# Two-layer graph attention on one core: other orders of the same instructions inside a tile's step

## What is computed

```python
h = jnp.maximum(_layernorm(x, axis=-1), 0.0)
x = x + _L0_gnn_ref(h, adj, L0_gnn_W, L0_gnn_a)   # scores leaky_relu(s1[:, None] + s2[None, :])
h = jnp.maximum(_layernorm(x, axis=-1), 0.0)
x = x + _L1_gnn_ref(h, adj, ...)                  # scores q @ k.T / sqrt(d)
# both: softmax over adj > 0, times the value rows, then elu
```

## Time and profile before

| | us |
|---|---|
| median of 3 runs | 2040.26 (2037.29 to 2045.88) |
| time of the profiled execution | 2041.44 |
| its span in the profile | 2039.7 |
| first phase | to about 1090 us |
| layer 1, even stretch | about 1180 to 2000 us |

### The profile page before, as it was taken

One profiled execution on the slowest core, in us unless ns is written; L12 is line 12 of the kernel. 1 busy time (PEld: TensorE's weight loads), 2 busy tenths in 40 slices (PEclk: granted clock), 3 DMA queues, 4 the chain that ended last, 5 costly groups with the idle time before them and its releaser, 6 DMA issues.

```text
span 2039.7 us, 23050 instructions
## 1 busy us (share of the span) xinstructions
PE 1260.7 (62%) x5314; PEld 968.6 (47%) x5362; DVE 1285.1 (63%) x6912; ACT 770.2 (38%) x1507; POOL 1130.4 (55%) x1206
## 2 busy tenths in 40 slices
PE   2756766766776676676653355666666665665566
PEld 1433444444444444444443245555555655555555
DVE  4556777767777777777775255565555565565555
ACT  2865566565656665656621011111111111111111
POOL 1345555555555555555563656666666666666661
PEclk9876777676677766767755566666665566666665
DMA  9788989998899998998621211222221222222121
GB/s 314 288 308 319 324 310 331 318 333 288 321 335 322 322 331 306 334 327 315 239 56 39 57 43 49 53 53 52 55 54 53 54 53 53 54 54 53 47 55 31
DMA packets 122262, 372.40 MB, mean 183 GB/s; under 512 B 34577, under 2 KB 67858, under 8 KB 89362
## 3 DMA queue, kind: packets, MB, share of 16 engines
q1 hardware_dynamic: 75458, 289.83, 38.7%
q0 software_dynamic: 38464, 81.08, 15.3%
q10 hardware_dynamic: 8208, 0.03, 0.2%
HBM read 358.12 MB, written 12.72 MB: 182 GB/s over the span
## 4 chain that ended last, share of the span: by engine, by line
DVE 46%; another core or an unknown queue 25%; PE 11%; issue 9%; ACT 5%; DMA 2%; SPq 1%; POOL 0%; DVEq 0%; ACTq 0%; POOLq 0%
DVE arena L873 8%; PE psum L1389 4%; DVE arena L699 3%; DVE arena L758 3%; ACT arena L1171 3%; DVE arena L761 2%; DVE arena L1120 2%; DVE arena L791 2%; DVE arena L866 2%; DVE arena L891 1%; DMA table<-arena 1%; PE psum L1526 1%; PE psum L1527 1%; DVE arena L1124 1%
## 5 line engine op out<-in xcount | busy, mean ns | idle before, releaser
L572 POOL DMA_INDIRECT arena<-table,arena x576 | 549.1, 953 | 432.9 <-DVE arena L827 269.7
L602 POOL DMA_INDIRECT arena<-table,arena x576 | 553.0, 960 | 335.1 <-DVE arena L882 165.5
L1171 ACT ACTIVATE arena<-arena 128x2048 bf16<-128x2048 int32 x256 | 485.4, 1897 | 26.1 <-DMA arena<-in_adj_dram 26.0
L1349 PE MATMUL psum<-arena 128*128 128x512 bf16 x976 | 331.8, 484 | 114.5 <-ACT arena L1171 59.2
L1396 PE MATMUL psum<-arena 128*128 128x131 f32 (+1 forms) x768 | 207.6, 442 | 302.5 <-DVE arena L866 274.3
L1396 PEld LDWEIGHTS psum<-arena 128*128 128x128 f32 x768 | 172.9, 324 | 317.2 <-issue 316.7
L873 DVE SCALAR_TENSOR_TENSOR arena<-arena 128x131 f32<-128x131 f32 (+1 forms) x768 | 268.5, 350 | 36.8 <-DVE arena L876 15.5
L1349 PEld LDWEIGHTS psum<-arena 128*128 128x128 bf16 x1024 | 116.8, 124 | 286.7 <-issue 177.7
L1306 ACT ACTIVATE arena<-psum 128x384 f32<-128x384 f32 x64 | 31.5, 492 | 493.5 <-remote 456.3
L1389 PEld LDWEIGHTS psum<-arena 128*128 128x128 f32 x768 | 148.2, 273 | 90.5 <-DVE arena L856 63.9
L1389 PE MATMUL psum<-arena 128*128 128x1 f32 x768 | 141.5, 300 | 66.5 <-DVE arena L856 52.4
(11 more groups left out here) (199 smaller groups left out, 2230.0 us busy)
## 6 DMA issues: line engine op xcount, KB each, us to landing
arena<-in_adj_dram SPq DMA_DIRECT2D x256, 1024.0 KB
arena<-table,arena POOLq DMA_INDIRECT x1152
table<-arena POOLq DMA_DIRECT2D x32, 132.0 KB, 5.3
arena<-table SPq DMA_DIRECT2D x64, 66.0 KB
table<-arena SPq DMA_DIRECT2D x16, 256.0 KB
arena<-table SPq DMA_DIRECT2D x64, 64.0 KB
out_dram<-arena SPq DMA_DIRECT2D x16, 256.0 KB
arena<-in_x_dram SPq DMA_DIRECT2D x4, 0.5 KB, 12.1
```

The lines of the kernel that those rows point to most:

```text
L572: pool.indirect_dma_start(Gt[:, v % GROUP, c + 1, :], None, table0, bass.IndirectOffsetOnAxis(idx_now[:, v % GROUP, c:c + 1], 0))\
L602: pool.indirect_dma_start(Gt[:, t % GROUP, c + 1, 0:D], None, table1, bass.IndirectOffsetOnAxis(idx_now[:, t % GROUP, c:c + 1], 0))\
L1171: nc.scalar.activation(mask[:, k, q * QUARTER:(q + 1) * QUARTER], adj_sb[:, k, q, :], ACT.Relu, accum_out=sum_all[:, bass.ds(tile, 1), q:q ...
L1349: nc.tensor.matmul(V[k], shifted[:, s, :], mask[:, k, s * 512:(s + 1) * 512], start=(s == 0), stop=False)
```

## The change

The same instructions run in other orders; none is added, removed or resized, and no transfer moves to another queue. In layer 1: VectorE runs `total` ahead of `maxima`; TensorE runs `scatter` right behind the transpose of the sums and the owners' six matmuls last; ScalarE copies the transposed sums first and the owners' product last. In the first phase: ScalarE copies the dealt list behind quarter 2 instead of ahead of it, and `prob_over` goes to the head of the next step; VectorE puts `below` behind `pick`, `finish` and `measure`, and `weigh` behind the next scores; TensorE runs `scatter` and the dealing ahead of `sum_up`.

```diff
@@ VectorE, first phase @@
                     u, v, w = t - LATE, t - PICK, t - DONE
-                    if live(t, DONE):
-                        weigh(w, w % 2, w % GROUP)
...
                         score0(u, u % 2, u % GROUP, u // GROUP + 1)
+                    if live(t, DONE):
+                        weigh(w, w % 2, w % GROUP)
...
-                    if live(t, LATE):
-                        below(u, u % 2)
                     if live(t, PICK):
                         pick(v, v % GROUP)
                     if live(t, DONE):
                         finish(w, w, w % 2)
                         measure(w, w % GROUP)
+                    if live(t, LATE):
+                        below(u, u % 2)
@@ VectorE, layer 1 @@
+                        if live(t, 3):
+                            total(T + t - 3, m, DE)
                         if live(t, 2):
                             maxima(T + t - 2, k, r)
-                        if live(t, 3):
-                            total(T + t - 3, m, DE)
@@ ScalarE, first phase @@
+                    if live(t, DONE):
+                        prob_over(w, w % 2)
                     quarter(1)
+                    quarter(2)
                     if live(t, PICK):
                         act.wait_ge(deal_done, v + 1)
                         nc.scalar.activation(owned_list[:, v % GROUP, :, :], deal_ps[v % 2], ACT.Identity).then_inc(owned_done, 1)
-                    quarter(2)
...
-                    if live(t, LATE):
-                        prob_over(u, u % 2)
@@ TensorE, first phase @@
-                    if live(t, DONE):
-                        at_least(pe, summed, w - 1)
-                        sum_up(w, w % 2, w % GROUP, D + 3)
                     if live(t, LATE):
                         scatter(u, u % 2, u % GROUP)
...
                         last.then_inc(deal_done, 1)
+                    if live(t, DONE):
+                        at_least(pe, summed, w - 1)
+                        sum_up(w, w % 2, w % GROUP, D + 3)
```

More of the change, by code:

```diff
@@ L1303, in attend @@
                               .then_inc(accn_done, 1)
-                        if live(t, 1):
-                            act.wait_ge(own_done, t)
-                            nc.scalar.activation(owned[:, (b - 1) % GROUP, :, :], own_ps[(b - 1) % 2], ACT.Identity)\
-                              .then_inc(owned_done, 1)
+                            act.wait_ge(acc_turned, t - 3)
+                            nc.scalar.activation(accT[:, k, :], accT_ps[k], ACT.Identity).then_inc(accT_done, 1)
                         if live(t, 0):
@@ L1310, in attend @@
                             nc.scalar.activation(h_col[:, b % 2, :], h_col_ps, ACT.Identity).then_inc(h_col_sb, 1)
-                        if live(t, 4):
-                            act.wait_ge(acc_turned, t - 3)
-                            nc.scalar.activation(accT[:, k, :], accT_ps[k], ACT.Identity).then_inc(accT_done, 1)
-                        if live(t, 2):
-                            prob_rows(T + t - 2, k)
                         if live(t, 4):
@@ L1320, in attend @@
                         if live(t, 2):
+                            prob_rows(T + t - 2, k)
                             prob_over(T + t - 2, k)
+                        if live(t, 1):
+                            act.wait_ge(own_done, t)
+                            nc.scalar.activation(owned[:, (b - 1) % GROUP, :, :], own_ps[(b - 1) % 2], ACT.Identity)\
+                              .then_inc(owned_done, 1)
                 unrolled(attend, G + 1)
@@ L1508, in attend @@
                             nc.tensor.transpose(accT_ps[k], accn[:, k, :], ident[:, :]).then_inc(acc_turned, 1)
+                        if live(t, 2):
+                            scatter(T + t - 2, k, r)
+                        if live(t, 0):
+                            pe.wait_ge(self_in[b], 16 * (G + g + 1))
+                            at_least(pe, u_kept, t)
+                            nc.tensor.transpose(h_col_ps, Gt[:, b, 0, 0:D], ident[:, :]).then_inc(h_col_done, 1)
+                        if live(t, 4):
+                            pe.wait_ge(accT_done, t - 3)
+                            nc.tensor.matmul(o_ps[k], accT[:, k, :], proj[:, 1, :], start=True, stop=False)
+                            nc.tensor.matmul(o_ps[k], ones[0:1, 0:P], bvrow[0:1, :], start=False, stop=True).then_inc(o_done, 1)
+                        if live(t, 0):
+                            pe.wait_ge(h_col_sb, t + 1)
+                            nc.tensor.matmul(u_ps, h_col[:, b % 2, :], mix[:, 1, :], start=True, stop=True).then_inc(u_done, 1)
+                        if live(t, 2):
+                            spread_max(T + t - 2, k, r)
                         if live(t, 1):
@@ L1517, in attend @@
                             last.then_inc(own_done, 1)
-                        if live(t, 0):
-                            pe.wait_ge(self_in[b], 16 * (G + g + 1))
-                            at_least(pe, u_kept, t)
-                            nc.tensor.transpose(h_col_ps, Gt[:, b, 0, 0:D], ident[:, :]).then_inc(h_col_done, 1)
-                        if live(t, 2):
-                            scatter(T + t - 2, k, r)
-                        if live(t, 4):
-                            pe.wait_ge(accT_done, t - 3)
-                            nc.tensor.matmul(o_ps[k], accT[:, k, :], proj[:, 1, :], start=True, stop=False)
-                            nc.tensor.matmul(o_ps[k], ones[0:1, 0:P], bvrow[0:1, :], start=False, stop=True).then_inc(o_done, 1)
-                        if live(t, 0):
-                            pe.wait_ge(h_col_sb, t + 1)
-                            nc.tensor.matmul(u_ps, h_col[:, b % 2, :], mix[:, 1, :], start=True, stop=True).then_inc(u_done, 1)
-                        if live(t, 2):
-                            spread_max(T + t - 2, k, r)
                 unrolled(attend, G + 1)
```

## The result

The changed kernel takes 2178.93 us (2175.77 to 2182.32) against 2038.78 us (2035.83 to 2045.88), a ratio of 1.0682 with a 95% interval of 1.0649 to 1.0716: slower by 140 us (139 by the ratio). The profiled execution has a span of 2180.6 us, 140.9 more than before.

What follows compares the result with a forecast made beforehand. Layer 1 was taken as a loop of waits on TensorE results held during gathers, the first phase as several resources near their limit. 2041.4 - 63 (layer 1) - 15 (first phase) = 1963, forecast 1960 us, range 1885 to 2130.

Steps and rivals of the forecast that it cites:

- What bounds the kernel now: Layer 1: TensorE results finished late in nine gathers arrive about 1.9 us after the last; loop 13.8 us a tile.
- The limit at x = 6.5: Layer 1: TensorE results finished before 6.5 us into a run of gathers get through; later ones are held.
- The change in layer 1: Layer 1: two tiles take 25.4 us, a tile 12.7 instead of 13.75; 63 us off over 60 tiles.
- It is released at 11.2 + 1.9 = 13.1, if the next run doesn't matter.: Layer 1: `scatter`, held from x = 7.5, comes 1.9 us behind its run's gathers, 1.5 us into the next run.
- Rival (c): Layer 1: gather runs without a pause make it slower, 2075 us in a small case or 2200 in a large; chance 0.32.
- large case: Layer 1: a hold lasts through a second run, 16.7 us a tile, 180 us slower, 2200 us; chance 0.15.
- Rival (a): Layer 1: no hold in the new order, GpSimd bounds at 11.55 us a tile; 1880 us in all; chance 0.16.
- Rival (b): Layer 1: `total` held in every tile through `sum_up`, step 13.6 us, no change that can be told, 2030 us; chance 0.22.
- The change in the first phase: First phase: buffers come free sooner and VectorE's wait at L860 shrinks; 15 us off, between 0 and 60.
- The new wait at `weigh`: First phase: `weigh` waits for `prob_over`, now behind a mask; 1.2 us shows in every second tile.
- The range: Whole kernel: 1885 to 2130 us, leaving out the best half of (a) and most of the large case of (c).

Runs made afterwards that it cites:

- A: First stage of the staged kernel, held: layer 1 with all orders as in the kernel before; 13.6 us a tile.
- the staged kernel: Changed kernel with layer 1 cut into six stages, each with its own orders or gathering stops; held, 2120.9 us beside 2020.3 of the kernel before.
- D: Stage of the staged kernel, held: against the orders before, only TensorE's and ScalarE's new orders in layer 1; 16.3 us a tile.
- E: Stage of the staged kernel, held: changed orders, and gathers of tile t also wait for `below` of tile t - 3; 16.2 us a tile.
- the other three held traces: Changed kernel with gathers also waiting for `maxima` (2159.7 us), the staged kernel (2120.9), and seven stages with pauses or no gathers (1946.0).

## Why the prediction was wrong

**What bounds the kernel now** held up: in the held condition a pause decides when TensorE's late results arrive, and A of the staged kernel has the step of before, 13.6 us. The limit at x = 6.5 was drawn too sharp, and time in the run alone doesn't set it. `scatter` at x = 6.2 came 2.3 us late in D, so there is a stretch in which results are late but not held; `spread_max` at x = 7.9 came 1.3 us late in E. What decides between the two stays open.

**The change in layer 1.** The first half of the sum came out: owners at 4.6 (4.4 in the sum), `sum_up` at 5.9 (6.0), next run at 11.3 without a pause (11.55); only `total` was at 9.2 instead of 7.9, which cost nothing. The step that failed is "It is released at 11.2 + 1.9 = 13.1, if the next run doesn't matter." The next run matters: 1474.01 in the timeline, x = 19.95 and not 13.1. What follows from 13.1, a pause of some 2.7 us in every second tile and 12.7 us a tile, fell with it: the pause in every second tile is 10.8 us. Measured: 16.55 us and a loss of 163.8 us where 63 off were forecast.

**Rival (c)** was what happened, in its large case: 33.4 us for two tiles worked out, 33.1 measured, 2200 us against 2179. It is right in its place and size, and partly by luck in its way: I had `scatter` held to 24.7 and everything behind it free. It came at 19.95, and `spread_max` was then held to 25.7. I gave this case 0.15. Its evidence, the joined runs of the earlier trace rows with a hold to 5.9 us behind four tiles' gathers, was the only row of layer 1 that showed joined runs. I overlooked that the first phase has two runs of eighteen (127.78 to 177.56 us), and that `scatter` and the dealt lists came 3.0 us behind the second of them. There they had ended only near its end, so they say nothing of a hold that lasts through a second run. What I set against it, that a held `sum_up` makes a pause, assumed the release at 13.1 that was in question.

**Rival (a)** describes the free condition: GpSimd's 11.5 us a tile. The Trainium skill, "SBUF — State Buffer", section "SBUF: two separate sides", has TensorE and ScalarE wait for nobody at their ports. The free traces agree (11.5 us a tile, both orders the same). In the held ones a result of TensorE came 13.1 us late (6.8 to 19.95 above); no run shows whether a port of the SBUF has to do with it. The kernel before has this rate in the free condition too, so it is no gain of the change.

**Rival (b)** did not occur: `total` was never held in every tile.

**The change in the first phase.** 15 us were forecast, the first gather of layer 1 came 22.9 us earlier. The wait of VectorE at L860 fell from 84.8 us to 0.7, as said, while 32.4 us came up at L882. The new wait at `weigh` (L866) didn't come. ScalarE's waits for the dealt lists fell from 236.7 to 60.8 us; its waits at L1202 rose from 92.6 to 148.6. But SyncE's wait for masks, which was to fall under 300 us, rose:

```profile
SPq L448 <- ACT arena L1171: 399.3, 125, 17.1
```

So the buffers didn't come free sooner in the way that I had worked out. The first phase alone was timed only in the free condition (no difference); that it is worth 23 us by itself where results are held isn't shown. What speaks for it: the other three held traces, all with the changed first phase, begin layer 1 at 1084.9 to 1097.9 us, and only the kernel before at 1124.7.

**The range** of 1885 to 2130 us left the large case of (c) out on purpose; it was the case that came.

## What to carry to other kernels

When a wait is taken away, ask what its pause let through: here `total` behind `maxima` looked like a false dependency, and it was what separated the runs of gathers. A sum that rests on "if the next run doesn't matter" is a sum over two cases, and the row that shows the other case, however odd its place, sets the chance. Change orders within one trace, stage by stage, when the condition of the chip can't be chosen, and look at the kernel before in the same condition first.

## What the runs showed of the hardware that was not expected

- The same kernel takes 2020 to 2040 us in one condition and 1713 to 1717 in the other, and the difference is in how late results of TensorE reach VectorE and ScalarE while indirect gathers are issued. What sets the condition wasn't found; one chip showed both.
- In the held condition, in eighteen gathers in a row a result of TensorE came 13.1 us late (x = 6.8 to 19.95), and one of the next, `spread_max`, 3.5 us behind the last gather; in runs of nine it came 1.9 us behind it. With a pause of 3.2 us between runs GpSimd never waited for `total`, with one of 1.2 us it did in every second tile, and one of 1.8 us in the middle of a run gave the shortest step, 12.9 to 13.3 us. Each figure is read from one execution.
- Waiting for five gathers to land costs 1.6 us a tile in layer 1 of the free condition (13.1 against 11.5).
